# A bias folded, a row moved to TensorE and norms in two passes, in a dense feed-forward stage

## The reference

```python
h = _layernorm(attended + x, ln1_scale, ln1_bias)
ff = jax.nn.relu(h @ W1 + b1) @ W2 + b2
return _layernorm(ff + h, ln2_scale, ln2_bias)
```

## Time and profile before

| what | value |
|---|---|
| median of three runs | 2275.96 us (2274.62 to 2282.95) |
| the profiled execution | 2270.11 us, its span 2268.0 us |
| TensorE busy over the span | 2064.1 us, 91% |
| VectorE busy | 1348.2 us, 59% |
| GpSimd busy | 730.7 us, 32% |
| ScalarE busy | 726.7 us, 32% |
| the chain that ended last, by engine | PE 58%, DVE 17%, POOL 11% |

### The profile page before, as it was taken

How to read it: one execution, slowest core, us unless ns; L and a number is a source line. 1 busy time by engine, 2 the same in 40 slices (tenths; PEclk the granted TensorE clock), 3 DMA queues, 4 the chain that set the end, 5 groups by cost and what they waited for, 6 DMA issues and landing times.

```text
span 2268.0 us, 31396 instructions
## 1 busy us (share of the span) xinstructions
PE 2064.1 (91%) x11980; PEld 1260.4 (56%) x11980; DVE 1348.2 (59%) x3189; ACT 726.7 (32%) x1551; POOL 730.7 (32%) x508
## 2 busy tenths in 40 slices
PE   4998986888978898989999999999999999999977
PEld 3555554443325555546764457678677754455554
DVE  6665687877979997752224544341222243289997
ACT  4221122321015554422213355554111111135552
POOL 1346878887875635530000000000000000014443
PEclk9998998999999999999999999999999999999989
DMA  9994232223239987653000010004000014000000
GB/s 324 387 375 118 3 77 3 3 3 66 3 43 214 216 222 219 179 141 126 1 1 10 1 76 1 1 1 171 16 1 1 1 36 117 0 1 10 10 15 14
DMA packets 122053, 181.97 MB, mean 80 GB/s; under 512 B 67761, under 2 KB 69451, under 8 KB 118071
## 3 DMA queue, kind: packets, MB, share of 16 engines
q1 hardware_dynamic: 76833, 178.51, 24.9%
q0 software_dynamic: 45072, 1.46, 5.6%
HBM read 109.21 MB, written 70.71 MB: 79 GB/s over the span
## 4 chain that ended last, share of the span: by engine, by line
PE 58%; DVE 17%; POOL 11%; issue 5%; ACT 4%; DMA 3%; SPq 2%; DVEq 0%; PEldq 0%; ACTq 0%; POOLq 0%; PEld 0%
PE banks L204 17%; POOL edge_table L623 11%; PE banks L2400 6%; PE banks L2442 6%; DVE arena L1450 4%; PE banks L1751 3%; PE banks L2228 2%; PE banks L2216 2%; PE banks L2203 2%; PE banks L1550 2%; PE banks L2826 2%; DMA edge_table<-arena 2%; PE banks L2252 2%; PE banks L1571 2%; PE banks L198 2%
## 5 line engine op out<-in xcount | busy, mean ns | idle before, releaser
L623 POOL DMA_INDIRECT edge_table<-arena x313 | 525.4, 1678 | 256.6 <-DMA edge_table<-arena 153.6
L204 PE MATMUL banks<-arena 128*125 128x512 f32 x1200 | 554.9, 609 | 15.4 <-DVE arena L3046 14.3
L204 PEld LDWEIGHTS banks<-arena 128*125 128x125 f32 x1200 | 221.4, 193 | 261.1 <-issue 243.9
L2853 POOL CAST arena<-arena 125x128 f32<-125x128 uint32 x10 | 2.9, 292 | 699.3 <-DVE arena L2989 699.2
L1450 DVE TENSOR_TENSOR arena<-banks,arena 125x1000 f32<-125x1000 f32 x100 | 193.6, 1952 | 36.6 <-ACT banks L1529 19.7
L2348 DVE SCALAR_TENSOR_TENSOR arena<-banks,arena 125x512 f32<-125x512 f32 x80 | 60.1, 751 | 189.4 <-PE banks L2442 189.4
L2095 DVE CUSTOM_DVE_ANT_0 arena<-banks,arena 125x512 f32<-125x512 f32 (+8 forms) x144 | 73.0, 553 | 128.9 <-PE banks L2203 126.1
L2400 PEld LDWEIGHTS banks<-arena 128*128 128x128 f32 x1280 | 144.0, 192 | 6.7 <-issue 6.6
L1550 PE MATMUL banks<-arena 64*125 64x250 f32 x800 | 113.2, 402 | 37.1 <-DVE arena L1450 33.5
L2400 PE MATMUL banks<-arena 128*128 128x125 f32 x1280 | 146.4, 276 | 0.1
L2442 PE MATMUL banks<-arena 128*125 128x512 f32 x320 | 139.2, 593 | 0.0
(11 more groups left out here) (372 smaller groups left out, 3394.0 us busy)
## 6 DMA issues: line engine op xcount, KB each, us to landing
edge_table<-arena SPq DMA_DIRECT2D x23, 2304.0 KB, 26.2
arena<-edge_table SPq DMA_DIRECT2D x100, 326.8 KB
arena<-edge_table SPq DMA_DIRECT2D x50, 330.8 KB
arena<-L_ffn_W SPq DMA_DIRECT2D x4, 2048.0 KB, 10.2
adjacency<-arena SPq DMA_DIRECT2D x50, 109.4 KB
arena<-adjacency SPq DMA_DIRECT2D x10, 546.9 KB
edge_table<-arena POOLq DMA_INDIRECT x313
arena<-edge_table SPq DMA_DIRECT2D x100, 37.9 KB
```

The lines of the kernel that those rows point to most:

```text
L204: last = nc.tensor.matmul(dst, xT[:, i, :], w[:, i, 0:n], start=(i == 0), stop=(i == k - 1))
L623: pool.indirect_dma_start(d["table"], bass.IndirectOffsetOnAxis(ap=cell[0:EP, c:c + 1].bitcast(U32), axis=0), vals[0:EP, c * ROW:(c + 1) * ...
```

## The change

It does four things. (1) ln1's bias is no longer added to h in the norm. Its effect on the hidden layer, W1^T ln1_bias, is put into the first layer's bias: four small products turn the row into columns, eight more multiply it with W1, and ScalarE adds b1. (2) Its effect on h itself, and b2, are added by TensorE: one product per half row accumulates `ln1_bias + b2` in the bank of the W2 product. (3) Norms take two passes instead of three: (h - mean) * scale, then * rstd; in `finish` the second pass also adds X. (4) From tile 4 on, ScalarE takes the first pass as rstd * h - mean * rstd, and VectorE only multiplies by the scale. The two bias rows are no longer spread and copied.

```diff
-        MIX_BIASES, BIASES = 9, 13
+        MIX_BIASES, BIASES, BIAS_ROWS = 7, 11, 13
...
         def mix_dve(dve):
+            nc.vector.tensor_tensor(both_rows[0:2 * BIAS_ROWS, :], ident[0:2 * BIAS_ROWS, 2 * LN1_ROW:2 * LN1_ROW + 2],
+                                    ident[0:2 * BIAS_ROWS, 2 * B2_ROW:2 * B2_ROW + 2], ALU.add)
...
+            link(dve, nc.vector.scalar_tensor_tensor(out=minus_mean[0:TP, :], in0=mv[0:TP, :, 0], scalar=-1.0,
+                                                     in1=rstd[0:TP, :], op0=ALU.mult, op1=ALU.mult))
             def normed(t):
                 h = Hm[0:TP, t, :]
-                link(dve, normalize(h, h, t))
-                link(dve, nc.vector.tensor_tensor(h, h, ln1_s[0:TP, :], ALU.mult))
-                nc.vector.tensor_tensor(h, h, ln1_b[0:TP, :], ALU.add).then_inc(m_h1, 1)
+                if t < NORMED_DVE:
+                    link(dve, nc.vector.scalar_tensor_tensor(out=h, in0=h, scalar=mv[0:TP, t, 0:1], in1=ln1_s[0:TP, :],
+                                                             op0=ALU.subtract, op1=ALU.mult))
+                    nc.vector.tensor_scalar(h, h, rstd[0:TP, t:t + 1], None, ALU.mult).then_inc(m_h1, 1)
+                else:
+                    dve.wait_ge(m_act, 4 + t - NORMED_DVE + 1)
+                    nc.vector.tensor_tensor(h, h, ln1_s[0:TP, :], ALU.mult).then_inc(m_h1, 1)
...
-                link(dve, nc.vector.tensor_tensor(h, bank(5 + t % 2)[0:TP, :], h, ALU.add))
-                nc.vector.tensor_tensor(h, h, b2_m[0:TP, :], ALU.add).then_inc(m_g, 1)
+                nc.vector.tensor_tensor(h, bank(5 + t % 2)[0:TP, :], h, ALU.add).then_inc(m_g, 1)
...
         def mix_act(act):
+            def normalized(t):
+                act.wait_ge(m_h1, 1)
+                h = Hm[0:TP, t, :]
+                nc.scalar.activation(h, h, ACT.Identity, scale=rstd[0:TP, t:t + 1],
+                                     bias=minus_mean[0:TP, t:t + 1]).then_inc(m_act, 1)
+            act.wait_ge(m_act, 1)
+            nc.scalar.activation(ln1_col, bank(2)[:, 0:KC], ACT.Copy).then_inc(m_act, 1)
+            act.wait_ge(m_act, 3)
+            for m in range(2):
+                last = nc.scalar.activation(b1_both[:, m:m + 1], bank(3)[:, m:m + 1], ACT.Identity, bias=b1_m[:, m:m + 1])
+            last.then_inc(m_act, 1)
             hT(0)
             hT(1)
+            for t in range(NORMED_DVE, NORMED_DVE + 2):
+                normalized(t)
...
+                if t + NORMED_DVE + 2 < TILES:
+                    normalized(t + NORMED_DVE + 2)
...
         def mix_pe(pe):
-            unused_products(bank(2), wo_m[:, 0, :], 5)
+            def fold_bias():
+                for k in range(KC):
+                    row, half = 2 * LN1_ROW + k // 2, k % 2
+                    last = nc.tensor.matmul(bank(2)[:, k:k + 1], bias_rows[:, 128 * half:128 * half + 128],
+                                            ident[0:2 * BIAS_ROWS, row:row + 1], start=True, stop=True)
+                last.then_inc(m_act, 1)
+                pe.wait_ge(m_act, 2)
+                for m in range(2):
+                    for k in range(KC):
+                        last = nc.tensor.matmul(bank(3)[:, m:m + 1], w1_m[:, k, m * 128:(m + 1) * 128], ln1_col[:, k:k + 1],
+                                                start=(k == 0), stop=(k == KC - 1))
+                last.then_inc(m_act, 1)
+            def bias_products(dst):
+                for half in range(2):
+                    nc.tensor.matmul(dst[:, C // 2 * half:C // 2 * (half + 1)],
+                                     both_rows[0:2 * BIAS_ROWS, half:half + 1].to_broadcast([2 * BIAS_ROWS, TP]), bias_rows,
+                                     start=(half == 0), stop=False, skip_group_check=True)
+            fold_bias()
+            pe.wait_ge(m_act, 4)
+            unused_products(bank(2), wo_m[:, 0, :], 4)
...
-                pe.wait_ge(m_r1, t + 1)
                 if t >= 2:
                     pe.wait_ge(m_g, t - 1)
-                project(bank(5 + t % 2)[0:TP, :], f1_m[t % 2], w2_m, k=2).then_inc(m_f2, 1)
+                bias_products(bank(5 + t % 2)[0:TP, :])
+                pe.wait_ge(m_r1, t + 1)
+                for k in range(2):
+                    last = nc.tensor.matmul(bank(5 + t % 2)[0:TP, :], f1_m[t % 2][:, k, :], w2_m[:, k, :], start=False,
+                                            stop=(k == 1), skip_group_check=True)
+                last.then_inc(m_f2, 1)
...
             def finish(t):
-                link(dve, normalize(h, h, t))
-                link(dve, nc.vector.tensor_tensor(h, h, ln2_s[0:TP, :], ALU.mult))
-                link(dve, nc.vector.tensor_tensor(X[0:TP, t, :], X[0:TP, t, :], h, ALU.add))
+                link(dve, nc.vector.scalar_tensor_tensor(out=h, in0=h, scalar=mv[0:TP, t, 0:1], in1=ln2_s[0:TP, :],
+                                                         op0=ALU.subtract, op1=ALU.mult))
+                link(dve, nc.vector.scalar_tensor_tensor(out=x, in0=h, scalar=rstd[0:TP, t:t + 1], in1=x,
+                                                         op0=ALU.mult, op1=ALU.add))
```

More of the change, by code:

```diff
@@ L294, in gps_two_layers @@
         s_scat = [sem(f"columns_scattered_{v}") for v in range(2)]
-        MIX_BIASES, BIASES = 9, 13
+        MIX_BIASES, BIASES, BIAS_ROWS = 7, 11, 13
+        SPREAD_ROWS = (0, 1, 2, 3, 4, 7, 8, 9, 10, 11, 12)
         BIAS_BANKS = (3, 5, 6, 7)
@@ L307, in spread_bias @@
             for half in range(2):
-                r = 2 * i + half
+                r = 2 * SPREAD_ROWS[i] + half
                 last = nc.tensor.matmul(bias_bank(i)[0:TP, half * C // 2:(half + 1) * C // 2],
-                                        ident[0:2 * BIASES, r:r + 1].to_broadcast([2 * BIASES, TP]), bias_rows,
+                                        ident[0:2 * BIAS_ROWS, r:r + 1].to_broadcast([2 * BIAS_ROWS, TP]), bias_rows,
                                         start=True, stop=True)
@@ L567, in edges_act @@
             weight_part(act, 0, False)
-            rows_m = (bq_m, bk_m, bv_m, bo_m, ln1_s, ln1_b, b2_m, ln2_s, ln2_b)
+            rows_m = (bq_m, bk_m, bv_m, bo_m, ln1_s, ln2_s, ln2_b)
             for i in range(4):
@@ L671, in gps_two_layers @@
         space = Space(BUF, KEYS_AT)
-        bq_m, bk_m, bv_m, bo_m, b2_m = (space.take(C) for _ in range(5))
-        ln1_s, ln1_b, ln2_b = (space.take(C) for _ in range(3))
+        bq_m, bk_m, bv_m, bo_m = (space.take(C) for _ in range(4))
+        ln1_s, ln2_b = (space.take(C) for _ in range(2))
         b1_m = space.take(2)
@@ L679, in gps_two_layers @@
         rd_m = space.take(8)
-        bias_rows = space.take(C // 2)[0:2 * BIASES, :]
+        bias_rows = space.take(C // 2)[0:2 * BIAS_ROWS, :]
         ln2_s = space.take(C)
+        ln1_col, b1_both = space.take(KC), space.take(2)
+        both_rows = space.take(2)
+        minus_mean = space.take(TILES)
+        LN1_ROW, B2_ROW = 5, 6
+        NORMED_DVE = 4
         f1_m = [chunks(k_m[:, 2 * TP * v:2 * TP * (v + 1)], TP, 2) for v in range(2)]
@@ L706, in gps_two_layers @@
         m_g = sem("mix_ff_added")
+        m_act = sem("mix_bias_folding_then_rows_normalized")
         def mix_sp(sp):
@@ L802, in mix_dve @@
             ln_stats_dve(dve, Hm, 1e-6, gathered=True)
+            link(dve, nc.vector.scalar_tensor_tensor(out=minus_mean[0:TP, :], in0=mv[0:TP, :, 0], scalar=-1.0,
+                                                     in1=rstd[0:TP, :], op0=ALU.mult, op1=ALU.mult))
             def normed(t):
                 h = Hm[0:TP, t, :]
-                link(dve, normalize(h, h, t))
-                link(dve, nc.vector.tensor_tensor(h, h, ln1_s[0:TP, :], ALU.mult))
-                nc.vector.tensor_tensor(h, h, ln1_b[0:TP, :], ALU.add).then_inc(m_h1, 1)
-            for t in range(4):
+                if t < NORMED_DVE:
[5 more added lines that the diff above has]
+                    nc.vector.tensor_tensor(h, h, ln1_s[0:TP, :], ALU.mult).then_inc(m_h1, 1)
+            for t in range(NORMED_DVE):
                 normed(t)
             for t in range(TILES):
-                if t + 4 < TILES:
-                    normed(t + 4)
+                if t + NORMED_DVE < TILES:
+                    normed(t + NORMED_DVE)
                 dve.wait_ge(m_f2, t + 1)
@@ L871, in hT @@
                 nc.scalar.activation(xT_m[t % 2], chunks(bank(t % 2)[:, :], TP), ACT.Copy).then_inc(m_hT, 1)
+            def normalized(t):
[9 more added lines that the diff above has]
+            last.then_inc(m_act, 1)
             hT(0)
             hT(1)
+            for t in range(NORMED_DVE, NORMED_DVE + 2):
+                normalized(t)
+            act.wait_ge(m_act, 4)
             for t in range(TILES):
@@ L880, in mix_act @@
                     last = nc.scalar.activation(f1_m[t % 2][:, m, :], bank(2 + t % 2)[:, m * TP:(m + 1) * TP],
-                                                ACT.Relu, bias=b1_m[:, m:m + 1])
```

(1 more changed line is left out.)

2 lines of the change are left out of this document (1 added, 1 removed).

## The result

The changed kernel takes 2280.58 us (median of 20 runs, 2271.27 to 2290.0), the kernel before 2274.03 us (20 runs, 2267.9 to 2282.95). The medians lie 6.6 us apart. The ratio is 1.003, with a 95% interval of 1.0017 to 1.0043, which is 3.9 to 9.8 us more. In a later set of twelve runs it was 1.0029 (1.0012 to 1.0046). The forecast, 2279.5 us, is 1.1 us from the measured median, but part of that is luck: it stood on a median of 2275.96 us for the kernel before, from three runs, and twenty give 2274.03. As a difference it was +3.6 us. The direction was right and the change stayed under 0.5%, but the measured one is nearly twice as large and the forecast lies just under its interval. Its profiled execution took 2271.27 us, with a span of 2269.5 us. That is the shortest of its executions, so the two profiled times (1.2 us apart) can't show the change; the stage's own rows can.

A forecast was written before the change was run, and what follows sets the result against it. VectorE set the feed-forward stage's pace; after the change TensorE would. Start 5.5 us later, loop and tail 1.9 back, graph stage nothing: +3.6 on 2275.96 gives 2279.5 us, forecast range 2273.5 to 2284, overall 2270 to 2288.

The forecast's parts named there:

- Scatters are not the bound, delays pass through: Edge attention starts when the graph stage's own engines are done, so the feed-forward stage's +3.6 us travels there.
- scatter rival: GpSimd's edge scatters bound the kernel and the stage's time is worth nothing; 2273 to 2276 us, chance 0.10.
- Start of the stage: Feed-forward stage before its first W2 product: small bias products and waiting for ScalarE make that product 5.5 us later.
- TensorE becomes the bound: Feed-forward loop: a pair of tiles costs TensorE 11.1 us against VectorE's 8.6, so TensorE sets the pace.
- The loop and tail: From first W2 product to the stage's end: 57.2 us instead of 59.1, giving 1.9 us back.
- VectorE's passes: VectorE in the feed-forward stage: about 18 us of work leaves it; two-input passes taken at 0.69 us.
- first rival: VectorE stays the measure, stage up to 15 us shorter, table loads waiting for scatters cap the gain; 2261 to 2272 us, chance 0.09.
- clock rival: TensorE's clock stays at 1.2 GHz into the feed-forward loop; +25 us with half the loop so, 2301 us, chance 0.06.

The follow-up runs named there:

- extra unused products: Kernel before with fifteen unused products at the start of the stage instead of five; ratio to the kernel before 1.0035 (1.0019 to 1.0051).
- early fold, row on VectorE: Changed kernel with the bias preparation moved ahead of last sums and square root, and the bias row added by VectorE; ratio to before 0.9997, again 0.9990.

## Why the forecast held

*Scatters are not the bound, delays pass through.* Right. The extra unused products moved the whole, and over these thirteen traces the first table load stands 292 to 297 us behind the stage's end. The scatter rival's premise came true in part (1.61 us a scatter instead of 1.70) and its time, 2273 to 2276 us, did not.

*Start of the stage, forecast +5.5.* Right in mechanism, 6.1 measured against the mean of three traces. That it came so close is luck in part. The forecast put the first W2 product 16.6 us behind the square root (324.7 - 308.14), and it came after 18.3 and 18.0, some 1.6 later; but the trace it started from has 11.1 us there, and the three average 12.0. The eight small products took 3.58 us (3.8 forecast). The unused ones ended 10.5 and 10.2 us behind the square root instead of 9.2: the clock was granted at 0.50 until 311.3 us, where I had let it rise 6 us after the small products began; they didn't bring it up as I took it. The windows are (311.3 follows from the 0.83):

```profile
310.00:311.00 1.00, 1.00 (x2) 0.38 (x2) 0.00 (x0) 0.00 (x0) 1.00 (x1) 0.50 0.10 2
311.00:312.00 1.00, 1.00 (x3) 0.33 (x2) 0.00 (x0) 0.00 (x0) 0.69 (x2) 0.83 0.39 4
312.00:313.00 1.00, 1.00 (x9) 0.76 (x7) 0.00 (x0) 0.13 (x1) 0.93 (x1) 1.00 0.06 1
```

The row's product then cost 1.05 instead of 0.93, and the other small terms 0.3 more.

*TensorE becomes the bound.* Right, by three experiments: without the row 50 us behind the first W2 product, with it 60.13 in each kernel with the new norms.

*The loop and tail, forecast -1.9.* This is the step that was off: the measured value is +0.1 against the mean, and +1.0 against the trace it started from. The mis-sized term is the row, 0.93 us a tile forecast and **1.24 measured**. The ninth W2 product came 46.5 us behind the first instead of 43.6. Of these 2.9 us 8 x 0.31 = 2.5 are the row, and 0.4 is the turn that the ninth tile lacks, which I had counted off and which saved nothing (36.5 us without the row, where the same sum gives 36.2). The 13.6 us from there to the end were as forecast. The 1.24 are 1.05 for the four records (0.26 each, 0.23 in the row that I priced it by), 0.10 by which the W2 product beside it grew (1.98 against 1.88), and 0.09 ahead of it (from L1033 to the next product 1.93 instead of 1.84). The rule on small contractions in the Trainium skill, "TensorE: Matmul & The Clock Gate", "Why this matters for your kernels", stands: 26 rows deep cost even a little more than the row I priced it by, and nowhere near 26/128.

*VectorE's passes.* Two-input passes 0.75 instead of 0.69, ScalarE's normalising 0.80 instead of 0.6. Both were off the path.

*The first rival's cap.* Its mechanism was right, its size half right. I had 4 us of lead use up the room; leads of 6.65 (no row) and 8.6 us were kept in full, and one of 8.7 and one of 11.7 lost 6 to 7 us. The last scatter did not follow the lead by a fixed share as I had it: with 8.6 and 8.7 us it started 0.3 and 5.8 us later than in the kernel before.

*The clock rival* didn't happen: 0.97 from the first W2 product on.

## What to carry to other kernels

Before work is moved from the engine that sets the pace, count the second engine's own period: here TensorE stood at 9.24 us a pair and VectorE at 12.75 (2 x 3.94 + 4.87); VectorE fell below 9, and two short products a tile put TensorE at 11.73. A one-off preparation belongs where its engine already waits, ahead of the instruction that ends the wait and not behind it: the same fold cost 6 us in one place and nothing in the other. And a stage's gain is worth only what the next deadline leaves: measure the room before working for more, and more than once: here block 25 let 8.6 us of lead through in one execution and 2.6 of 8.7 in another.

## What the runs showed of the hardware

*The same wait is followed by a lower clock in one execution and not in another.* In the edge attention TensorE waits 2.35 us for VectorE. In the kernel before the products after it ran at full speed:

```profile
867.44 1.11 PE L1550 MATMUL banks<-arena 64*125 64x250 f32 x8 [2.35 <-DVE arena L1450]
868.39 0.38 PE L1556 MATMUL banks<-arena 64*125 64x250 bf16 x4
868.70 1.06 PE L1571 MATMUL banks<-arena 125*64 125x250 f32 x8
```

In the kernel without the row, behind the same wait of the same length, they did not:

```profile
861.21 1.11 PE L1607 MATMUL banks<-arena 64*125 64x250 f32 x8 [2.35 <-DVE arena L1507]
862.16 0.38 PE L1613 MATMUL banks<-arena 64*125 64x250 bf16 x4
862.47 1.75 PE L1628 MATMUL banks<-arena 125*64 125x250 f32 x8
```

From 850 to 995 us that kernel's granted clock was 0.95 against 1.00, and of a lead of 6.65 us at block 27 none was left at block 49 (994.98 against 994.61 us). The times of the runs go with the clock too: one and the same kernel (early fold, row on VectorE) took 2261 to 2269 us at a mean clock of 0.974 and more, and 2277 to 2282 at 0.967 and less. A gain of a few microseconds is smaller than that and shows only in a stage's own rows, or in many runs.

*The scatters' pace varies from execution to execution.* In the two executions of the early fold with the row on VectorE the first table load left at 662.25 and 661.75 us, and the last of the 313 scatters at 804.51 and 810.00; in the changed kernel it left at 805.25 and 798.70. What sets it is open.
